# Two-stage graph and expert kernel: the first six expert tiles run inside the last graph steps, and VectorE waits for a store two tiles back

## The reference, cut to what matters

```python
def reference(x, adj, ...):                       # x: 128 graphs x 128 nodes x 128 features, float32
    x = x + gnn(layernorm(x), adj, ...)           # agg = eps*x + adj@x; silu(rmsnorm(agg@W1 + b1)) @ W2 + b2
    x = x + ffn(layernorm(x), ...)
    return x

def ffn(x, gate_w, gate_b, w1, b1, w2, b2, gamma, beta):   # 16 experts, hidden 256, 2 experts per row
    topk_vals, topk_idx = top_k(x @ gate_w + gate_b, 2)
    topk_w = softmax(topk_vals)
    h = relu(x @ w1[e] + b1[e])                   # e: the two experts of the row
    moe = sum(topk_w * (h @ w2[e] + b2[e]))
    y = x + moe
    return (y - mean(y)) / sqrt(var(y) + 1e-5) * gamma + beta
```

## Time and profile before

| | us |
|---|---|
| median of 3 runs | 845.04 |
| lowest, highest | 844.89, 848.12 |
| the profiled execution: its own time | 846.69 |
| its span, first to last instruction | 844.9 |
| TensorE busy | 737.2 |
| VectorE busy | 625.5 |
| ScalarE busy | 528.4 |
| GpSimd busy | 519.3 |

### The profile page before, as it was taken

The page is one execution under the profiler, slowest core; times in us unless marked ns, Lnnn a source line. Parts: engine busy times, 40 slices in busy tenths (PEclk is TensorE's granted clock), DMA queues, the critical chain, the costliest instruction groups (busy, mean ns, idle before and its releaser), DMA issues. The chain is left out here.

```text
span 844.9 us, 18953 instructions
## 1 busy us (share of the span) xinstructions
PE 737.2 (87%) x4709; PEld 570.2 (67%) x4710; DVE 625.5 (74%) x2290; ACT 528.4 (63%) x1123; POOL 519.3 (61%) x540
## 2 busy tenths in 40 slices
PE   4899999999999999995289999999999999998700
PEld 3577777787787777874167777777777777776500
DVE  2589999999999998886657666567776776666664
ACT  2589999999999999985223333355545445444441
POOL 3004777776677777767540067767777773777774
PEclk9799999999999999998579999999999999999955
DMA  5365555555555553221465577778888887888632
GB/s 160 117 227 193 176 167 176 190 190 191 182 173 177 167 174 121 74 82 53 118 195 150 156 204 197 211 206 225 235 229 229 225 225 206 225 231 223 196 109 81
DMA packets 141531, 149.20 MB, mean 177 GB/s; under 512 B 18835, under 2 KB 113059, under 8 KB 141222
## 3 DMA queue, kind: packets, MB, share of 16 engines
q1 hardware_dynamic: 122614, 111.13, 43.5%
q0 software_dynamic: 16384, 34.11, 14.2%
q10 hardware_dynamic: 2480, 3.40, 1.3%
HBM read 83.02 MB, written 65.55 MB: 176 GB/s over the span
## 5 line engine op out<-in xcount | busy, mean ns | idle before, releaser
L482 POOL DMA_INDIRECT dispatched<-rows,slot_i x256 | 258.3, 1009 | 169.1 <-issue 160.7
L501 POOL DMA_INDIRECT work<-results,place x184 | 182.7, 993 | 118.7 <-DVE tout L1200 63.2
L817 ACT ACTIVATE hid<-bank,wts 128x256 f32<-128x256 f32 x286 | 119.9, 470 | 212.1 <-PE bank L681 210.2
L1200 DVE SCALAR_TENSOR_TENSOR tout<-bank,gate,tin 128x128 f32<-128x128 f32 x286 | 87.2, 346 | 119.3 <-PE bank L696 118.4
L696 PE MATMUL bank<-w_all,hid 128*128 x1144 | 165.9, 288 | 0.0
L681 PE MATMUL bank<-tut,wts 128*128 128x256 f32 x572 | 150.0, 386 | 6.9 <-DVE tut L1183 6.9
L696 PEld LDWEIGHTS bank<-w_all,hid 128*128 128x128 f32 x1144 | 138.7, 191 | 17.2 <-issue 0.2
L533 PEld LDWEIGHTS bank<-w_sb,work 128*128 128x128 f32 x1024 | 123.2, 194 | 17.6 <-issue 14.6
L533 PE MATMUL bank<-w_sb,work 128*128 128x128 f32 x1024 | 126.4, 278 | 1.6 <-ACT work L796 1.6
L527 PE MATMUL bank<-agg,w_sb 128*128 128x512 f32 x256 | 125.2, 612 | 0.0
L681 PEld LDWEIGHTS bank<-tut,wts 128*128 128x128 f32 x572 | 98.6, 193 | 16.4 <-DVE tut L1183 8.1
(11 more groups left out here) (186 smaller groups left out, 1049.3 us busy)
## 6 DMA issues: line engine op xcount, KB each, us to landing
tin<-dispatched SPq DMA_DIRECT2D x143, 132.0 KB
wts<-in_w_exp SPq DMA_DIRECT2D x143, 129.0 KB
results<-tout SPq DMA_DIRECT2D x26, 704.0 KB, 5.2
results<-tout SPq DMA_DIRECT2D x143, 128.0 KB
xs<-in_x SPq DMA_DIRECT2D x32, 256.0 KB, 3.3
adj_sb<-in_adj_t SPq DMA_DIRECT2D x32, 256.0 KB
rms_b<-r_row SPq DMA_DIRECT2D x32, 256.0 KB, 3.5
out<-agg SPq DMA_DIRECT2D x32, 256.0 KB
```

What stands on the lines that cost most here:

```text
L482: nc.gpsimd.indirect_dma_start(dispatched, bass.IndirectOffsetOnAxis(slot_i[:, k, n:n + 1], 0), rows[:, k, n // TOPK, n % TOPK, :], None). ...
L501: nc.gpsimd.indirect_dma_start(moe_of(g)[:, n // TOPK, n % TOPK, :], None, results, bass.IndirectOffsetOnAxis(place[:, g, n:n + 1], 0)).th ...
L817: last = nc.scalar.activation(hid[:, n % 2, c, :], hid_ps[n % 2][:, c * TILE:(c + 1) * TILE], ACT.Relu, bias=wts[:, k, F + c:F + c + 1], s ...
L1200: last = nc.vector.scalar_tensor_tensor(out=tout[:, k, a, :], in0=exp_ps[n % 2][:, a * D:(a + 1) * D], scalar=gate[:, n % 2, a:a + 1], in1 ...
```

## The change

`LAG` goes from 3 to 2. `FIRST` goes from 9 to 10, and the choice of the first tiles uses the counts after 22 groups (`EARLY_AT`): two sets of four small matmuls in step 25, a copy, and six parts of `early_tiles`, one in each of the steps 26 to 31 on VectorE. `first_table` has six entries. The tile steps of tiles 0 to 5 are written between the graph steps `NG`, `NG`+1 and `NG`+2 and between the parts of the lists, on TensorE, ScalarE and VectorE, by hand. What was `first_tiles` is cut into `early_tiles`, `tiles_by_then` and `lists_of_tiles`; the totals keep their instructions. SP's order is as before, with 22 groups' scatters to wait for in place of 29. VectorE's outputs 0 to 5 have no wait for a store; output 6 waits for the stores of tiles 0 to 4.

```diff
-FIRST = 9
+FIRST = 10
+EARLY_AT = 22
+EARLY_STEP = EARLY_AT + 3
-LAG = 3
+LAG = 2
...
             for k in range(RING):
-                sp.wait_ge(scattered[k], 16 * GB * TOPK * len(range(k, FULL_AT, RING)))
+                sp.wait_ge(scattered[k], 16 * GB * TOPK * len(range(k, EARLY_AT, RING)))
...
+                if i is None and t == EARLY_STEP:
+                    pe.wait_ge(hist_done, EARLY_AT)
+                    for q, upto in enumerate((SEGS[0], EARLY_AT)):
+                        for j in range(GB):
+                            last = nc.tensor.matmul(q_ps[:, (4 + q) * E:(5 + q) * E], ones_b[:], hist[:, upto - 1, j, :],
+                                                    start=(j == 0), stop=(j == GB - 1))
+                    last.then_inc(early_done, 1)
...
+            step(None, NG)
             pe.wait_ge(x1_done, NG)
-            pe.wait_ge(table_done, 1)
+            pe.wait_ge(z_done, HC * NG)
+            pe.wait_ge(rb_out, NG)
+            pe.wait_ge(first_done, 1)
...
+            tile_step(None, -1)
+            tile_step(None, 0)
+            step(None, NG + 1)
+            tile_step(None, 1)
+            step(None, NG + 2)
+            tile_step(None, 2)
...
+            tile_step(None, 3)
+            tile_step(None, 4)
+            pe.wait_ge(cols_done, 1)
...
+            tile_step(None, 5)
+            pe.wait_ge(table_done, 1)
+            pipeline(pe, tile_step, RING2, P2[1], P2[2], P2[3], RING2)
...
+            step(None, NG)
+            tile_step(None, 0)
+            step(None, NG + 1)
+            tile_step(None, 1)
+            step(None, NG + 2)
+            for t in range(2, 5):
+                tile_step(None, t)
+            act.wait_ge(pad_done, 1)
...
+                if i is None and EARLY_STEP < t < NG:
+                    early_tiles(t - EARLY_STEP - 1)
...
-                    if n >= LAG:
+                    if i is None and n == RING2:
+                        for k in range(RING2 - LAG):
+                            dve.wait_ge(t_kept[k], 16)
+                        k = n % RING2
+                    if n >= RING2:
                         dve.wait_ge(t_kept[(n - LAG) % RING2], count(i, (n - LAG) // RING2 + 1, 16, 1))
...
+            step(None, NG)
+            tile_step(None, -1)
+            step(None, NG + 1)
+            tile_step(None, 0)
+            tiles_by_then()
+            tile_step(None, 1)
+            step(None, NG + 2)
+            tile_step(None, 2)
+            lists_of_tiles()
+            tile_step(None, 3)
+            totals()
+            tables()
+            dve.wait_ge(u_done, NG)
+            dve.wait_ge(slots_done, NG)
+            tile_step(None, 4)
+            places(None, 0)
+            tile_step(None, 5)
```

More of the change, by code:

```diff
@@ L636, in step @@
                     last.then_inc(past_done, 1)
[L638 to L656, removed]
+            pipeline(pe, step, *P1[:3], NG)
             def tile_step(i, t):
@@ L660, in tile_step @@
                 if has(i, n, NT):
-                    e = pe.value_load(table[0:1, bass.ds(count(i, n, 1, RING2), 1), 1], min_val=0,
+                    listed = first_table if i is None and n < RING2 else table
+                    e = pe.value_load(listed[0:1, bass.ds(count(i, n, 1, RING2), 1), 1], min_val=0,
                                       max_val=(E - 1) * D)
@@ L798, in step @@
                             half_gap(t - 3)
[L800 to L807, removed]
+            pipeline(act, step, *P1[:3], NG)
             def tile_step(i, t):
@@ L820, in tile_step @@
                     last.then_inc(t_relu, 1)
+            step(None, NG)
[6 more added lines that the diff above has]
+            act.wait_ge(pad_done, 1)
+            _, starts = nc.values_load_multi_w_load_instructions(
+                pad_row[0:1, E // 2:E], engines=[mybir.EngineType.Activation], min_val=0, max_val=E * CAP)
+            for r in starts:
+                act.dma_start(pad_rows(r), pad[:]).then_inc(padded, 16)
+            tile_step(None, 5)
             def normalise(g, half):
@@ L931, in first_tiles, with lists_of_tiles @@
                         float(TILE - 1), None, ALU.add))
-                link(nc.vector.tensor_scalar(nt_i[:, 0, 10:11], past[:, FULL_AT - 1:FULL_AT], 0.0, None, ALU.add))
-                link(nc.vector.tensor_single_scalar(nt_i[:, 1, 0:NS - 1], nt_i[:, 0, 0:NS - 1],
+                link(nc.vector.tensor_single_scalar(nt_i[:, 1, 0:NS - 2], nt_i[:, 0, 0:NS - 2],
                                                     TILE.bit_length() - 1, op=ALU.arith_shift_right))
[L935 to L947, removed]
+                link(nc.vector.tensor_copy(nt_f[:, 0:NS - 2], nt_i[:, 1, 0:NS - 2, :]))
+            def lists_of_tiles():
                 link(nc.vector.tensor_tensor(upto_t[:, 2:NS, :], nt_f[:, 0:NS - 2, :],
@@ L1112, in step @@
                     dve.wait_ge(ms_done, count(i, g + 1))
+                    if i is None and t == EARLY_STEP:
+                        dve.wait_ge(early_done, 1)
+                        nc.vector.tensor_copy(early_c[:], q_ps[:, 4 * E:6 * E].rearrange("p (q e) -> p q e", e=E))\
+                            .then_inc(early_out, 1)
                     nc.vector.tensor_scalar(msv[:, g % RING], q_ps[:, 0:GB], b1_norm[:, 0:1], 0.0,
                                             ALU.add, ALU.max).then_inc(ms_out, 1)
[L1115 to L1116 removed]
```

151 lines of the change are left out of this document (98 added, 53 removed).

## The result

| | before | changed |
|---|---|---|
| median, lowest to highest, us | 845.39, 842.45 to 848.12 (7 runs) | 852.22, 850.33 to 854.59 (7 runs) |
| profiled execution: own time, span | 846.69, 844.9 | 852.5, 850.7 |
| SP's stores of tiles 0, 6, 136 | 433.70, 449.71, 786.74 | 434.06, 448.94, 794.08 |
| GpSimd's last gather | 834.41 | 840.12 |

The ratio is 1.0092 (95% interval 1.0070 to 1.0113): by it the change costs 7.8 us (5.9 to 9.6). Three of the five later sets of runs were disturbed: the kernel before itself took 1264 to 1276 us there; its graph stage was longer and its tiles stood nearly still while GpSimd gathered.

A forecast was written before the change was run, and what follows sets the result against it. SP's issue was taken to bound the expert stage. Terms +1.0, +0.9, +1.5 and -1.1 sum to +2.3 us: 849.0 on the profiled execution, 847.3 us as median of the runs; range 840 to 853.

The forecast's parts named there:

- Passage: Between graph and expert stages: totals at 423.5, 5.7 us later than before; first store at 434.7, 1.0 us later.
- the 1.0 us of the graph stage: Last graph steps: the sixth part of `early_tiles` stands ahead of the routing on VectorE, 1.0 us (0 to 1.7).
- held by the pads, totals + 10.1: SP's first store: eight pads, then 0.9 us for the next read, let it issue 10.1 us after the totals.
- To tile 6: From SP's first store to its store of tile 6: 16.9 us instead of 16.0, with TensorE restarting at 1.2 GHz.
- +1.0 and +0.9: Two terms of lateness: SP's first store 1.0 us later, then the stretch to tile 6's store 0.9 us longer.
- The wait for two tiles back: Expert stage: VectorE's lead over SP is capped at 2.4 us, costing SP's chain +1.5 us, mostly at six `places`.
- L: Time from a store's issue to its landing, taken as 2.8 us in the busy expert stage.
- my own rule: Cost of the two-back wait from SP's remaining lead: about 0 at L = 2.4, 3 to 5 us at 3.4.
- a rival: Stores hold VectorE ahead of outputs, delaying TensorE and SP, from L about 3.1: 850.8 to 853 us; chance 0.25.
- The rule from the Trainium skill: HBM access of 2 us at high load: L an estimated 4.2 us, the two-back term some 10 us.
- GpSimd's gain: End of kernel: counts one lower let the last gathers start sooner, limited by all stores, -1.1 us (0 to -1.2).
- SP as the bound: Expert stage: SP's list reads, one store and two loads per tile set the pace, 2.59 us a tile.

The follow-up runs named there:

- e2: The kernel before with only the wait for two tiles back (LAG 2, MIX_FROM kept): 849.38 us, ratio 1.0064.
- e1: The changed kernel with the wait for three tiles back again (LAG 3, FIRST 9), so the rebuilt passage alone: 849.67 us, ratio 1.0063.
- control: The kernel before, unchanged, run once more for a second profile: 846.50 us, ratio 1.0007.
- e10: The changed kernel's early counts alone, its six tiles behind the totals, FIRST 9, LAG 3: 842.86 us, ratio 0.9981.
- e12: The changed kernel with `places` between the copy and the output, ahead of the store wait: 848.64 us, ratio 1.0049.
- e3: The changed kernel with two unread filler matmuls on TensorE behind each `places` but the first: 856.25 us, ratio 1.0146.
- e4: The kernel before with the first weights of tiles 6 and up issued by ScalarE in place of SP: 831.93 us, ratio 0.9855.
- e11: The changed kernel with the first weights of tiles 6 and up issued by ScalarE in place of SP: 839.42 us, ratio 0.9942.

## Why the prediction failed, step by step

**Passage: right in time, one reason wrong.** VectorE in the changed kernel, the totals' first copy and the last list:

```profile
422.95 0.17 DVE L1198 COPY tot<-bank 128x16 f32<-128x16 f32 x1
...
431.11 0.33 DVE L1231 CAST table<-bank 1x143 int32<-1x143 f32 x1
```

Forecast 423.5, or 424.5 with the 1.0 us of the graph stage, measured 422.95; totals to last list 8.6, measured 8.5; first store 434.7, measured 434.06. But "held by the pads, totals + 10.1" was right by luck: the pads took 5.3 us instead of 5.99 and ended at 431.51, with the last list (431.44), and from there to the store it is 2.6 us, not the 0.9 that I gave the next read. Totals to store is 11.1 us, and the totals' earlier start hid it.

**To tile 6.** Forecast +16.9 from the first store, measured 14.9. I paced it by TensorE; in the trace SP waits for nothing there and paces it itself, six stores 2.36 to 2.77 us apart, then tile 6's, whose output was ready 0.8 us earlier. The clock did fall, as forecast: tile 6 on TensorE.

```profile
437.00 0.69 PE L670 MATMUL bank<-ident,tin 128*128 128x128 f32 x2 [5.92 <-DMA tin<-dispatched]
437.48 1.92 PE L681 MATMUL bank<-tut,wts 128*128 128x256 f32 x4
```

Over all profiles the start is 2.4 us later where +1.0 and +0.9 were forecast: as marks the two terms together hold. As time they are too small: the passage alone costs 5.3 us (3.3 to 7.3) by its ratio, and the sum has no term for what it costs beyond tile 6.

**The wait for two tiles back: the step that failed.** I gave it +1.5 us; by the ratio of e2 it costs 5.4, and in the changed kernel the stage is 6.5 to 8.1 us longer than in the two profiles of before, 5.4 longer than in e1. The landing time was not at fault: where it mattered L was 2.8 to 3.2 for my 2.8, and over all waits its median is 2.4, where by my own rule "it is about 0". The rule was wrong: I asked only whether SP still finds an output in time, so VectorE's idle time looked free as long as a lead remained. The sentence "VectorE's next copy is queued behind it, and TensorE and then SP wait for that" stands in a rival, but its price was set by SP's lead again, from 3.1 us of landing time on. What decides is the sum in VectorE's queue between two copies for TensorE: store wait, output, `places`, statistics. TensorE had no slack at a place already before (it stood idle for 1.29 us at tile 88). Of the 3.0 us that the four tiles there now take longer, 0.8 is more idle time, and the remaining 2.2 go with the lower clock level behind it, which the term does not have at all. The times of that rival, 850.8 at L = 3.4 and 853 at 3.8, are near the 852.2 measured; its place and its queue are right, its condition was met only at two of the places (3.1 and 3.2), and its price came from the wrong chain. The rule from the Trainium skill, "DMA: Bandwidth & Descriptors", section "Latency and other measured facts", which would have made L an estimated 4.2 us and the term 10 us, is not met in this trace: at a DMA share of 0.70 to 0.88 the store ahead of `places` landed in 2.8 us, and no output waited for a landing of over 3.7.

**GpSimd's gain.** Forecast -1.1. From output 142 to the last gather: 37.0, 35.8, 36.8 and 34.9 us in before, control, e1 and e10 (`LAG` 3), 34.7, 34.7, 34.9 and 32.5 in the changed kernel, e12, e2 and e3 (`LAG` 2); with the weights on ScalarE 39.6 (e4) and 38.1 (e11). The means are 1.9 and 1.5 us less, but e10 with `LAG` 3 lies among the others: the gain fits the forecast and is not clear of the scatter.

**SP as the bound** was right (e4), and that is where the missed gain lay: 11.7 us for moving one issue per tile.

**The outcome.** Forecast 847.3, measured 852.2; the sum was +2.3, and the medians differ by 6.8. With 5.4 to 8.1 in place of 1.5 the forecast would have been 851.2 to 853.9. That the measured time still lies within my range of 840 to 853 is luck: its upper end was the rival at L = 3.8.

## What to carry to other kernels

Before you tighten a wait, read what is queued behind it on the same engine and who needs that next; the lead of the queue that the wait protects is only half of the account. If a long piece of work stands in that queue, put it ahead of the wait: the same wait, 99 us of it in all, then left the stage's length as it was. And when one queue's issue is the bound, take an issue off it (11.7 us here) before filling idle time elsewhere.

## Not expected of the hardware

- In a stage where TensorE is otherwise busy, idle gaps of 1.4 to 3.1 us behind `places` brought its granted clock down to the lower level for 3 to 7 us; yet one of 2.58 us left it at 1.00, as did most of those of 1.4. With each fall in the two back and the changed kernel four tiles took 1.6 to 3.0 us longer. Two fillers of 128 x 256 did not prevent it.
- A store of 128 KB landed in 1.9 to 3.7 us within one stage of one kernel. The median of a page can rest on few of the stores: it says 2.1 where the outputs that cost waited for landings of 2.8 to 3.2.
- The same kernel took 845 us on one occasion and 1264 to 1276 us on others, with a median ratio of 1.0004 between equal kernels there. The ratio looks as sound as ever, yet with e4's edit and the early counts it was 0.999 where e4's edit alone had given 0.9855, and the tiles hardly ran beside the gathers there. Which engine binds has to be looked up again in each set of runs.
